# Gate h of a pair takes the reset state into its seven products, in a five-step gated graph network on one core

## The chip, the core and the metric

The kernel runs on one core of a Trainium2 chip. A core has five engines that run their own instruction streams and meet through semaphores: TensorE (PE in the profile: matrix products from SBUF into PSUM banks), VectorE (DVE), ScalarE (ACT), GpSimd (POOL) and SyncE (SP, which here issues most of the DMA transfers). The metric is the device time of one execution in microseconds (us), as a median over runs; lower is better.

## The reference, cut to what matters

The state has 2048 nodes with 256 features, and five steps of this loop run, followed by a small output layer and a layer norm:

```
s_in = state @ in_W.T + in_b;  s_out = state @ out_W.T + out_b
a_in = A @ s_in;  a_out = A.T @ s_out;  a = [a_in, a_out, state]
r = sigmoid(a @ r_W.T + r_b);  z = sigmoid(a @ z_W.T + z_b)
h = tanh([a_in, a_out, r * state] @ h_W.T + h_b)
state = (1 - z) * state + z * h
```

## The kernel before

The state is kept transposed (`state_t`, features on the partitions) in two feature halves of 128 and four chunks of 512 nodes. A float operand goes to PE as two fp16 parts, a high and a low one: ACT makes the high part, DVE the low part, and PE multiplies the three pairs high-high, high-low and low-high (`PASSES`). So each product of a 128x128 weight block with a 128x512 operand block is three matmuls.

Step 0 and the last two chunks of step 4 take the gates chunk by chunk (L1911). All other work takes two neighbouring chunks as a **pair**: (t, p) is step t, pair p, and there are seven of them, (1,0), (1,1), (2,0), (2,1), (3,0), (3,1) and (4,0). In a step, `group(t, g)` (L1792) makes the adjacency products of one direction and one pair by seven products P1 to P7 of 16 matmuls each in place of eight (the Strassen-Winograd scheme on 2x2 blocks); sums of their results, on ACT and DVE, give the operands `yop` (`y_sum`, `y_lo` L1390, `y_hi` L739).

`pair_gate(t, p, gate)` then makes the four PSUM tiles of gate r, z or h of a pair: two feature halves times two chunks, the tiles s = 0 to 3 of `PAIR_TILES`. It uses the same scheme on the weights: product y11 (called P1) into tile 0, t2 (P6) into tile 1, t1 (P5) into tile 2, t3 (P7) into tile 3, and then y21 into tile 0, y22 into tile 1 and t4 into tile 3. The inner dimension has three parts: the two adjacency results d = 0 and d = 1, and the state. For gates r and z, `pair_product` gives each of the seven products 3 state matmuls (L1924, from `sop`) and 6 matmuls of d = 0 and 1 (L1932), 63 in all. For gate h the third part is r * state. There the seven products hold only their 6 matmuls of d = 0 and 1, and `pair_state` (L1943) adds r * state to each of the four tiles by plain products, 6 matmuls per tile: 42 + 24 = 66.

Between the products the tiles are combined. ACT copies P1 (`pair_copy` L791), DVE adds (`pair_sum_u` L1553 after P6, `pair_sum_12` L1559 after P5, `pair_sum_22` L1564 and L1566 after P7), ACT writes the base of tile 3 (`pair_base_21` L795), and then the last products come. In gate h, tiles are finished in the order 1, 2, 0, 3 (`PAIR_ORDER[2]`). While PE makes gate z, ACT applies the sigmoid to gate r (L806), DVE multiplies by the state (`pair_reset` L1572), ACT makes the high part (`pair_reset_hi` L813) and DVE the low part (`pair_reset_lo` L1579). Gate h's banks are those of gate r: ACT seeds them with a bias term (`pair_seed` L783) and DVE adds the second term (`pair_degree` L1544) before PE may add to them (`s_c1`). After gate h, ACT applies the tanh (L806) and DVE updates the state (`pair_keep` L1587, `pair_update` L1596 and L1599).

At the end of a step (after pair p = 1) the new rows of the state are split (`rows_hi` L623, L631, L638; `row_sums` L1126 to L1131; `rows_lo` L1101, L1104, L1108) and SP transposes them by DMA into `xop` (`turn` L441), three parts for each chunk: part 0 after L1101, part 1 after L638, part 2 after L1108. Chunk 3 comes first, then chunk 2. The next step's `first_group` starts on the chunks 0 and 1, which are there, and meets waits for the parts of the chunks 3 and 2 at fixed places: its first five products with four operand pairs each (two for P7) are 36 matmuls; then come P1, P6 and P5 on chunk 3 and P1 on chunk 2. Its products also overwrite the banks of the gates just made: bank 0 held tile 1 of z, bank 3 tile 2, bank 2 tile 0, bank 7 tile 3, and bank 1 tile 3 of h. So P1, P5, P3 and P7 wait until z * h has read those (`s_zh`), and P6 until the tanh of tile 3 has (`s_act`).

Nothing is scheduled by a planner: each engine runs its instructions in the order in which they are written.

Of the kernel before, what the change touches and what calls it, by code (L numbers as in the profile page):

```python
# [19 lines left out]
FT = D // P  # L20
JT = N // P
CW = 512
# [33 lines left out]
PAIR_ORDER = ((0, 1, 2, 3), (1, 2, 0, 3), (1, 2, 0, 3))  # L56

# [12 lines left out]
def gnn_program(nc, x, x_t, adj, adj_t, io_w, gate_w, o_w, bias, o2_b, out):  # L70
    ctx = ExitStack()
    with ctx:
# [60 lines left out]
        h_pair = (sum_v, sum_1, sum_u, sum_u)  # L133
        xsum_b = pq_words[:, slot_words + 3 * CW:slot_words + 5 * CW]
# [21 lines left out]
        rs_pair = tmp[:, 4 * CW:8 * CW].bitcast(F16).rearrange("p (c s f n) -> p c s f n", c=2, s=2, f=FT)  # L156
# [65 lines left out]
        s_rs, s_rsh, s_rsl = sem("s_rs"), sem("s_rsh"), sem("s_rsl")  # L222
# [57 lines left out]
        def pair_index(t, p):  # L280
            return 2 * (t - 1) + p

# [88 lines left out]
        def _(sp):  # L371
# [170 lines left out]
        def _(act):  # L542
# [254 lines left out]
            def pair_act(t, p, gate, i):  # L797
# [4 lines left out]
                if gate < 2 and s == 2:  # L802
# [6 lines left out]
            def pair_reset_hi(t, p, i):  # L809
                s = PAIR_ORDER[0][i]  # L810
                f, c = PAIR_TILES[s]
                act.wait_ge(s_rs, FT * pair_at(t, p) + i + 1)
                nc.scalar.activation(rs_pair[:, c, 0, f, :], r_pair[:, s, :], ACT.Identity, scale=SIGX) \  # L813
                    .then_inc(s_rsh, 1)

            def pair_gates(t, p):
# [109 lines left out]
        def _(dve):  # L926
# [218 lines left out]
            def reset_lo(n, f):  # L1145
                dve.wait_ge(s_rsh, FT * n + f + 1)
# [3 lines left out]
            def keep_part(n, c, f):  # L1150
                dve.wait_ge(s_act, GT * n + 2 + f + 1)
                dve.wait_ge(s_rsl, FT * n + f + 1)
# [422 lines left out]
            def pair_reset_lo(t, p, i):  # L1575
                s = PAIR_ORDER[0][i]
                f, c = PAIR_TILES[s]
                dve.wait_ge(s_rsh, FT * pair_at(t, p) + i + 1)
                nc.vector.scalar_tensor_tensor(rs_pair[:, c, 1, f, :], r_pair[:, s, :], SIGX, rs_pair[:, c, 0, f, :],  # L1579
# [509 lines left out]
```

## Time and profile before

| | |
|---|---|
| median of 3 runs (lowest, highest) | 989.48 us (988.64, 991.54) |
| the profiled execution's own time | 987.27 us |
| its span, first to last instruction | 985.5 us, clock 0.997 of full speed |
| PE busy | 965.1 us (98%), 4480 matmuls |
| DVE busy | 735.6 us (75%) |
| ACT busy | 457.0 us (46%) |
| POOL busy | 35.8 us (4%) |

A matmul is shown 379 ns long, but the next one starts before it ends, so the busy time of PE tells that it had work and not how fast it went; how fast is read from the distance between starts. A timeline row gives the start, the length of the whole merged piece (for xN equal instructions), and in brackets how long the engine was idle before it and what released it.

### The profile page before, as it was taken

What the parts mean: (1) busy time and instruction counts of PE and PEld (TensorE: products, weight loads), DVE (VectorE), ACT (ScalarE), POOL (GpSimd) and SP (SyncE); (2) the same over time, 40 slices, a digit from 0 to 9 for tenths busy, and PEclk for the clock granted to TensorE, in tenths of its full rate; (3) what the DMA queues carried; (4) which work ended last, traced back from release to release, by engine and by line L of the source; (5) the groups of instructions that cost most, each with busy time, mean ns of one, the idle gap of its engine ahead of it and who ended that gap; (6) DMA issues with size and microseconds to landing.
All of it is one profiled execution on the core that took longest, in us unless ns stands there. A gap on an engine that the chain in (4) does not pass through costs nothing.

```text
span 985.5 us, 11893 instructions
## 1 busy us (share of the span) xinstructions
PE 965.1 (98%) x4480; PEld 441.2 (45%) x4480; DVE 735.6 (75%) x1157; ACT 457.0 (46%) x640; POOL 35.8 (4%) x43
## 2 busy tenths in 40 slices
PE   7999999999999999999999999999999999999995
PEld 3444444444444444444444444444444444445443
DVE  4999999888876688767668775876676687645756
ACT  4667665553354246433534552463345335412443
POOL 0311100000000000000000000000000100001100
PEclk9999999999999999999999999999999999999998
DMA  9999993324810454383035617601570681032101
GB/s 342 393 416 370 395 328 102 81 60 109 224 52 1 131 152 93 59 206 110 1 86 151 137 20 166 184 5 43 150 172 12 146 221 55 1 112 81 44 1 43
DMA packets 199784, 134.34 MB, mean 136 GB/s; under 512 B 62256, under 2 KB 191920, under 8 KB 195760
## 3 DMA queue, kind: packets, MB, share of 16 engines
q1 hardware_dynamic: 197424, 125.20, 44.1%
q0 software_dynamic: 2304, 8.39, 2.2%
q8 instruction: 36, 0.59, 0.2%
q14 instruction: 20, 0.16, 0.0%
HBM read 102.11 MB, written 16.78 MB: 121 GB/s over the span
## 4 chain that ended last, share of the span: by engine, by line
PE 91%; DVE 5%; ACT 2%; issue 1%; DMA 0%; ACTq 0%; SPq 0%; DVEq 0%
PE bank L1792 35%; PE bank L1932 19%; PE bank L1911 12%; PE bank L1717 11%; PE bank L1924 6%; PE bank L1943 4%; PE bank L1711 1%; PE bank L2003 1%; PE bank L2024 1%; ACT areg L739 1%; DVE pq_words L1354 0%; DVE pq_words L1347 0%; DVE pq_words L1341 0%; DMA pq_words<-in_gate_w 0%; DVE pq_words L1108 0%
## 5 line engine op out<-in xcount | busy, mean ns | idle before, releaser
L1792 PE MATMUL bank<-areg,xop_words 128*128 128x512 fp8e4 x1792 | 389.4, 379 | 0.8 <-DVE pq_words L1354 0.8
L1792 PEld LDWEIGHTS bank<-areg,xop_words 128*128 128x128 f16 x1792 | 174.9, 98 | 212.9 <-DVE pq_words L1354 2.7
L739 ACT ACTIVATE areg<-pq_words 128x512 f16<-128x512 f32 x90 | 56.3, 629 | 163.8 <-DVE pq_words L1354 62.7
L1932 PE MATMUL bank<-areg,pq_words 128*128 128x512 f16 x504 | 119.2, 379 | 0.7 <-DVE areg L1390 0.7
L1717 PE MATMUL bank<-areg,xop_words 128*128 128x512 fp8e4 x512 | 111.5, 379 | 1.8 <-ACT areg L555 1.8
L1932 PE MATMUL bank<-areg,w 128*128 128x512 f16 x378 | 90.9, 379 | 1.4 <-DVE areg L1390 1.4
L1390 DVE SCALAR_TENSOR_TENSOR areg<-pq_words,areg 128x512 f16<-128x512 f32 x90 | 62.2, 691 | 32.4 <-ACT areg L739 30.6
L1717 PEld LDWEIGHTS bank<-areg,xop_words 128*128 128x128 f16 x512 | 50.0, 98 | 62.4 <-issue 2.2
L1932 PEld LDWEIGHTS bank<-areg,pq_words 128*128 128x128 f16 x504 | 49.3, 98 | 60.4 <-DVE areg L1390 1.2
L565 ACT ACTIVATE areg<-tmp 128x2048 fp8e4<-128x2048 int32 x31 | 59.2, 1909 | 31.1 <-DMA tmp<-in_adj_t 17.2
L1911 PE MATMUL bank<-pq_words,w 128*128 128x512 f16 x288 | 65.4, 379 | 0.0
L1932 PEld LDWEIGHTS bank<-areg,w 128*128 128x128 f16 x378 | 36.9, 98 | 46.3 <-DVE areg L1390 1.9
L646 ACT ACTIVATE tmp<-bank,bias_sb,scal 128x512 f32<-128x512 f32 x36 | 27.8, 772 | 44.9 <-PE bank L1911 44.9
L1924 PE MATMUL bank<-sop_words,wss 128*128 128x512 f16 x168 | 45.4, 379 | 0.0
L1911 PEld LDWEIGHTS bank<-pq_words,w 128*128 128x128 f16 x288 | 28.2, 98 | 34.0
L806 ACT ACTIVATE bank<-bank,bias_sb,scal 128x512 f32<-128x512 f32 x56 | 40.1, 733 | 3.3 <-PE bank L1932 3.3
L1943 PE MATMUL bank<-tmp,w 128*128 128x512 f16 x168 | 39.7, 379 | 0.0
L795 ACT COPY bank<-pq_words 128x512 f32<-128x512 f32 x21 | 12.4, 590 | 58.2 <-DVE pq_words L1564 58.2
L537 POOL TENSOR_TENSOR areg<-areg,diag_words 128x256 f32<-128x256 f32 x16 | 13.0, 843 | 694.2 <-DMA areg<-in_x 694.2
L1596 DVE TENSOR_TENSOR pq_words<-bank,pq_words 128x512 f32<-128x512 f32 x28 | 19.3, 688 | 23.1 <-ACT pq_words L806 23.1
L1911 PE MATMUL bank<-sop_words,w 128*128 128x512 f16 x144 | 35.0, 379 | 0.9 <-DVE bank L1136 0.9
L1579 DVE SCALAR_TENSOR_TENSOR tmp<-tmp,scal 128x512 f16<-128x512 f32 x28 | 21.0, 751 | 17.7 <-ACT tmp L813 17.7
(214 smaller groups left out, 1208.3 us busy)
## 6 DMA issues: line engine op xcount, KB each, us to landing
areg<-kept_operands SPq DMA_DIRECT2D x112, 512.0 KB, 4.3
tmp<-in_adj_t SPq DMA_DIRECT2D x16, 1024.0 KB, 8.0
tmp<-in_adj SPq DMA_DIRECT2D x15, 1024.0 KB, 7.0
kept_operands<-xop_words POOLq DMA_DIRECT2D x11, 512.0 KB, 8.1
kept_operands<-areg SPq DMA_DIRECT2D x4, 1024.0 KB, 10.4
areg<-in_x SPq DMA_DIRECT2D x7, 512.0 KB, 6.1
kept_operands<-tmp POOLq DMA_DIRECT2D x5, 512.0 KB, 3.2
pq_words<-in_gate_w SPq DMA_DIRECT2D x6, 384.0 KB, 5.4
```

The source lines that it names most:

```text
L565: nc.scalar.activation(raw8[k // JT][:, k % JT, :], stage[:, k % STG, :], ACT.Copy, accum_out=degc[:, k // JT, k % JT:k % JT + 1], saturat ...
L646: nc.scalar.activation(dst[:, gi % FT, :], gate_bank[gi % 3][:, :], ACT.Tanh if gi >= 2 * FT else ACT.Sigmoid, bias=bias_sb[:, 4 + gi:5 + ...
L739: nc.scalar.activation(y_dst(t, g, name)[:, 0, :], src, ACT.Copy, scale=PSC).then_inc(s_yh, 1)
L806: nc.scalar.activation(h_pair[s] if gate == 2 else slot, slot, ACT.Tanh if gate == 2 else ACT.Sigmoid, bias=bias_sb[:, 4 + gi:5 + gi], sca ...
L1390: nc.vector.scalar_tensor_tensor(rows[:, 1, :], src, PSC, rows[:, 0, :], ALU.mult, ALU.subtract).then_inc(s_yl, 1)
L1579: nc.vector.scalar_tensor_tensor(rs_pair[:, c, 1, f, :], r_pair[:, s, :], SIGX, rs_pair[:, c, 0, f, :], ALU.mult, ALU.subtract).then_inc(s ...
L1717: return nc.tensor.matmul(dst[:, :], state_n[:, j, part, feat(f)], adj8[:, j, cols(c)], start=j == 0 and part == 0, stop=j == JT - 1 and p ...
L1792: last = nc.tensor.matmul(dst[:, :], xop[:, m // 2, operand_block(xo, part, m % 2), :], place8[:, mo, m, :], start=first and m == pairs[0] ...
L1911: last = nc.tensor.matmul(dst[:, :], w16[:, k, wp, feat(gi)], rhs, start=False, stop=i == KT - 1 and (wp, xp) == PASSES[-1], skip_group_ch ...
L1924: nc.tensor.matmul(dst[:, :], weights(2, wp), sop[:, Y_PLACE[name], xp, :], start=False, stop=False, skip_group_check=True)
L1932: last = nc.tensor.matmul(dst[:, :], weights(d, wp), yop[:, d, Y_PLACE[name], xp, :], start=False, stop=final and d == 1 and (wp, xp) == P ...
L1943: last = nc.tensor.matmul(pair_banks[2][s][:, :], w16[:, 2 * FT + k, wp, feat(2 * FT + f)], rs_pair[:, c, xp, k, :], start=False, stop=k = ...
```

## The change

The seven products of gate h each take a third part of 3 matmuls, as those of the gates r and z do, from seven operands of the reset state b = r * state: y11, y21 and y22 are three of its tiles, t1 = b12 - b11, t3 = b22 - b12, t2 = b22 - t1 and t4 = b21 - t2. `pair_state` is gone. DVE makes the four sums (`pair_reset_sum`), and high and low parts are made for six items in the order `RS_ORDER`, where t1 and t2 are one item of 1024 columns. The new operands lie in `tmp` and in two stretches of `areg` into which the rows of x are loaded for the residual at the end. So that load (`load_rest` 0 and 1) now waits for the last pair's gate h and stands behind `load_group(14)` in SP's order. In `first_group`, P6 moves behind P5 and P3. In gate r of pair (1,0) the opening products come in the order t3, y11, t2, t1. The keeps of DVE are interleaved with the sums of gate h.

```diff
+RS_ORDER = ("y11", "y22", "t12", "t3", "y21", "t4")
+        rs_at = {"y11": rs_block[:, 0], "y22": rs_block[:, 1], "y21": rs_block[:, 2], "t4": rs_block[:, 3],
+                 "t1": rs_t12[:, 0], "t2": rs_t12[:, 1], "t3": rs_t3}
...
                 if t == LAST:
...
-                    load_rest(0)
-                    load_rest(1)
                 for at in range(4 * (t - 1) + 1, 4 * t + 1):
+                    if at == 4 * LAST - 1:
+                        sp.wait_ge(s_gate, GT * (CH * LAST + 2))
+                        load_rest(0)
+                        load_rest(1)
...
             def pair_gates(t, p):            # ScalarE
...
-                for i in range(3):
+                pair_act(t, p, 0, 0)
+                pair_reset_hi(t, p, "y11")
+                for i in range(1, 4):
                     pair_act(t, p, 0, i)
-                    pair_reset_hi(t, p, i)
-                pair_act(t, p, 0, 3)
                 pair_copy(t, p, 1)
-                pair_reset_hi(t, p, 3)
+                pair_reset_hi(t, p, "y22")
+                pair_reset_hi(t, p, "t12")
+                pair_reset_hi(t, p, "t3")
+                pair_reset_hi(t, p, "y21")
                 pair_seed(t, p, 2, 0)
+                pair_reset_hi(t, p, "t4")
                 pair_base_21(t, p, 1)
...
             def first_group(t):              # TensorE
...
-                if t > 1:
-                    pe.wait_ge(s_act, GT * pair_at(t - 1, 1) + 12)
-                product(bank_b, at, XS2, MT2, early, final=False)
                 if t > 1:
                     pe.wait_ge(s_zh, zs + 2)
                 product(bank_e, at, XS1, MT1, early, final=False)
                 if t > 1:
                     pe.wait_ge(s_zh, zs + 3)
                 product(bank_c, at, XS4, M22, early, final=False)
+                if t > 1:
+                    pe.wait_ge(s_act, GT * pair_at(t - 1, 1) + 12)
+                product(bank_b, at, XS2, MT2, early, final=False)
...
             def pair_product(t, p, gate, dst, name, weights, final=False):
...
+                if gate == 2:
+                    half_name = "t12" if name in ("t1", "t2") else name
+                    pe.wait_ge(s_rsl, rs_before(pair_at(t, p)) + RS_ORDER.index(half_name) + 1)
+                    for wp, xp in PASSES:
+                        last = nc.tensor.matmul(dst[:, :], weights(2, wp), rs_at[name][:, xp, :], start=False,
+                                                stop=final and (wp, xp) == PASSES[-1], skip_group_check=True)
                 return last
-            def pair_state(t, p, s):
...
```

**PE in gate h of the first pair.** Bank 5 is tile 1, bank 6 tile 2, bank 4 tile 0 and bank 1 tile 3. Before, from the opening product t1 on:

```order
L1932 MATMUL bank6<-areg,pq_words 128x512 x6
L1932 MATMUL bank1<-areg,pq_words 128x512 x6
L1932 MATMUL bank5<-areg,pq_words 128x512 x6
L1943 MATMUL bank5<-tmp,w16 128x512 x6
L1943 MATMUL bank6<-tmp,w16 128x512 x6
L1932 MATMUL bank4<-areg,w16 128x512 x6
L1943 MATMUL bank4<-tmp,w16 128x512 x6
L1932 MATMUL bank1<-areg,w16 128x512 x6
L1943 MATMUL bank1<-tmp,w16 128x512 x6
```

In the changed kernel, from the same product on:

```order
L2000 MATMUL bank6<-areg,pq_words 128x512 x6
L2008 MATMUL bank6<-areg,wss 128x512 x3
L2000 MATMUL bank1<-areg,pq_words 128x512 x6
L2008 MATMUL bank1<-areg,wss 128x512 x3
L2000 MATMUL bank5<-areg,pq_words 128x512 x6
L2008 MATMUL bank5<-tmp,wss 128x512 x3
L2000 MATMUL bank4<-areg,w16 128x512 x6
L2008 MATMUL bank4<-tmp,w16 128x512 x3
L2000 MATMUL bank1<-areg,w16 128x512 x6
L2008 MATMUL bank1<-tmp,w16 128x512 x3
```

The reset state has moved from the end of each tile into every product. Tile 1 (bank 5) was complete 30 matmuls before the end of the gate, tile 2 24 and tile 0 12 before it; now both tile 1 and tile 2 are complete 18 before it, tile 0 9 before it.

**PE in `first_group` of step 2**, right behind gate h of pair (1,1), with the semaphores waited for. Before:

```order
L1792 MATMUL bank0<-areg,xop_words 128x512 [waits s_zh,s_place0,s_turn01,s_turn00]
L1792 MATMUL bank0<-areg,xop_words 128x512 x7
L1792 MATMUL bank1<-areg,xop_words 128x512 [waits s_turn21,s_act,s_turn20,s_place4,s_turn11,s_turn10]
L1792 MATMUL bank1<-areg,xop_words 128x512 x7
L1792 MATMUL bank3<-areg,xop_words 128x512 [waits s_place3,s_zh]
L1792 MATMUL bank3<-areg,xop_words 128x512 x7
L1792 MATMUL bank2<-areg,xop_words 128x512 [waits s_place2,s_zh]
L1792 MATMUL bank2<-areg,xop_words 128x512 x7
```

In the changed kernel:

```order
L1859 MATMUL bank0<-areg,xop_words 128x512 [waits s_zh,s_place0,s_turn01,s_turn00]
L1859 MATMUL bank0<-areg,xop_words 128x512 x7
L1859 MATMUL bank3<-areg,xop_words 128x512 [waits s_turn21,s_zh,s_turn20,s_place3,s_turn11,s_turn10]
L1859 MATMUL bank3<-areg,xop_words 128x512 x7
L1859 MATMUL bank2<-areg,xop_words 128x512 [waits s_place2,s_zh]
L1859 MATMUL bank2<-areg,xop_words 128x512 x7
L1859 MATMUL bank1<-areg,xop_words 128x512 [waits s_place4,s_act]
L1859 MATMUL bank1<-areg,xop_words 128x512 x7
```

The product that waits for the tanh of tile 3 (bank 1, `s_act`) has moved from the 9th matmul to the 25th. What follows, and the places of the later waits for the transposes, is as it was.

**DVE while PE makes gate z of the first pair.** L1572 is `pair_reset`, L1579 `pair_reset_lo`, L1553 and L1559 are the sums after P6 and P5. Before:

```order
L1572 TENSOR_TENSOR tmp<-bank4,state_t 128x512
L1579 SCALAR_TENSOR_TENSOR tmp<-tmp,scal 128x512
L1572 TENSOR_TENSOR tmp<-bank5,state_t 128x512
L1579 SCALAR_TENSOR_TENSOR tmp<-tmp,scal 128x512
L1572 TENSOR_TENSOR tmp<-bank6,state_t 128x512
L1579 SCALAR_TENSOR_TENSOR tmp<-tmp,scal 128x512
L1572 TENSOR_TENSOR tmp<-bank1,state_t 128x512
L1553 TENSOR_TENSOR pq_words<-bank0,pq_words 128x512
L1579 SCALAR_TENSOR_TENSOR tmp<-tmp,scal 128x512
L1559 TENSOR_TENSOR bank0<-bank3,pq_words 128x512
```

In the changed kernel (L1605 is `pair_reset`, L1635 `pair_reset_lo`, L1586 and L1592 the two sums, L1615 to L1625 `pair_reset_sum`):

```order
L1605 TENSOR_TENSOR tmp<-bank4,state_t 128x512
L1635 SCALAR_TENSOR_TENSOR tmp<-tmp,scal 128x512
L1605 TENSOR_TENSOR tmp<-bank5,state_t 128x512
L1615 TENSOR_TENSOR pq_words<-tmp 128x512
L1605 TENSOR_TENSOR tmp<-bank6,state_t 128x512
L1618 TENSOR_TENSOR pq_words<-tmp 128x512
L1621 TENSOR_TENSOR pq_words<-tmp,pq_words 128x512
L1605 TENSOR_TENSOR tmp<-bank1,state_t 128x512
L1586 TENSOR_TENSOR pq_words<-bank0,pq_words 128x512
L1592 TENSOR_TENSOR bank0<-bank3,pq_words 128x512
L1635 SCALAR_TENSOR_TENSOR tmp<-tmp,scal 128x512
L1625 TENSOR_TENSOR tmp<-tmp,pq_words 128x512
```

Up to the sum after P5 the same number of instructions stands: three low parts have made way for three sums, and the low parts come later, between the seeds' second terms of gate h.

## Rows read from the trace of the kernel before

**Rows 1.** The page: span, engines, and the plain state products of gate h.

```profile
span 985.5 us, 11893 instructions
PE 965.1 (98%) x4480; PEld 441.2 (45%) x4480; DVE 735.6 (75%) x1157; ACT 457.0 (46%) x640; POOL 35.8 (4%) x43
...
L1943 PE MATMUL bank<-tmp,w 128*128 128x512 f16 x168 | 39.7, 379 | 0.0
```

**Rows 2.** Chain that ended last: a stretch of gate products.

```profile
393.15 7.77 PE bank L1932 x36
```

**Rows 3.** Timeline of PE, opening of gate r of pair (1,0).

```profile
274.87 0.81 PE L1924 MATMUL bank<-sop_words,w 128*128 128x512 f16 x3
...
277.75 0.82 PE L1932 MATMUL bank<-areg,w 128*128 128x512 f16 x3 [1.43 <-DVE areg L1390]
...
280.53 0.82 PE L1932 MATMUL bank<-areg,pq_words 128*128 128x512 f16 x3 [0.66 <-DVE areg L1390]
```

**Rows 4.** Timeline of DVE beside it.

```profile
274.75 1.75 DVE L1465 TENSOR_TENSOR pq_words<-tmp,pq_words 128x1536 f16<-128x1536 f32 x1
...
277.01 0.68 DVE L1390 SCALAR_TENSOR_TENSOR areg<-bank,areg 128x512 f16<-128x512 f32 x1
...
279.78 0.69 DVE L1390 SCALAR_TENSOR_TENSOR areg<-pq_words,areg 128x512 f16<-128x512 f32 x1 [0.69 <-ACT areg L739]
...
283.58 0.69 DVE L1559 TENSOR_TENSOR bank<-bank,pq_words 128x512 f32<-128x512 f32 x1
```

**Rows 5.** Timeline of PE, pair (1,1): gate z begins, gate h inside, step 2 begins.

```profile
380.69 0.81 PE L1924 MATMUL bank<-sop_words,w 128*128 128x512 f16 x3
...
392.99 2.75 PE L1932 MATMUL bank<-areg,w 128*128 128x512 f16 x12
...
408.53 20.88 PE L1792 MATMUL bank<-areg,xop_words 128*128 128x512 fp8e4 x96
```

**Rows 6.** Timeline of DVE, pair (1,1), during gate z.

```profile
379.02 0.68 DVE L1572 TENSOR_TENSOR tmp<-bank,state_t 128x512 f32<-128x512 f32 x1
...
387.59 0.69 DVE L1559 TENSOR_TENSOR bank<-bank,pq_words 128x512 f32<-128x512 f32 x1
```

**Rows 7.** Timeline of ACT, pair (1,1): last sigmoid of r, first and last tanh of h.

```profile
384.65 0.73 ACT L806 ACTIVATE bank<-bank,bias_sb,scal 128x512 f32<-128x512 f32 x1
...
402.26 0.78 ACT L806 ACTIVATE pq_words<-bank,bias_sb,scal 128x512 f32<-128x512 f32 x1 [1.28 <-PE bank L1943]
...
409.03 0.76 ACT L806 ACTIVATE pq_words<-bank,bias_sb,scal 128x512 f32<-128x512 f32 x1
```

**Rows 8.** Timeline of DVE, pair (1,1): updates of the state and low parts.

```profile
403.07 0.69 DVE L1596 TENSOR_TENSOR pq_words<-bank,pq_words 128x512 f32<-128x512 f32 x1 [1.98 <-ACT pq_words L806]
...
409.58 1.28 DVE L1108 SCALAR_TENSOR_TENSOR pq_words<-diag_words,scal,pq_words 128x1024 f16<-128x1024 f32 x1
```

**Rows 9.** Transposes of chunk 3 part 2 (issued 410.9) and chunk 2 part 0 (412.9).

```profile
L441 SPq DMA_TRANSPOSE xop_words<-pq_words x1: 1350/1350/1350, 410.9 to 410.9; - x1
DMA to landing us min/median/max: 3.4/3.4/3.4
...
L441 SPq DMA_TRANSPOSE xop_words<-tmp x1: 1232/1232/1232, 412.9 to 412.9; - x1
DMA to landing us min/median/max: 3.0/3.0/3.0
```

**Rows 10.** The same part 2 of chunk 3 at the end of step 3; PE's step 4 begins.

```profile
L441 SPq DMA_TRANSPOSE xop_words<-pq_words x1: 1349/1349/1349, 770.8 to 770.8; - x1
DMA to landing us min/median/max: 3.7/3.7/3.7
...
768.40 0.81 PE L1792 MATMUL bank<-areg,xop_words 128*128 128x512 fp8e4 x3
```

**Rows 11.** POOL's additions to the rows of x; a DVE split behind pair (4,0).

```profile
784.38 5.50 POOL L537 TENSOR_TENSOR areg<-areg,diag_words 128x256 f32<-128x256 f32 x8 [554.97 <-DMA areg<-in_x]
...
862.19 2.48 DVE L1076 SCALAR_TENSOR_TENSOR sop_words<-state_t,scal,sop_words 128x1024 f16<-128x1024 f32 x2 [1.22 <-ACT sop_words L594]
```

More of the change, by code:

```diff
@@ L133, in gnn_program @@
         h_pair = (sum_v, sum_1, sum_u, sum_u)
+        rs_sums_12 = pq_words[:, slot_words:slot_words + 2 * CW].rearrange("p (i n) -> p i n", i=2)
         xsum_b = pq_words[:, slot_words + 3 * CW:slot_words + 5 * CW]
@@ L281, in pair_index, with rs_before @@
             return 2 * (t - 1) + p
+        def rs_before(n):
+            t, c = n // CH, n % CH
+            if t == 0:
+                return FT * n
+            pairs = 2 * (t - 1) + (1 if c >= 2 else 0)
+            return FT * CH + len(RS_ORDER) * pairs + (FT * (c - 2) if t == LAST and c > 2 else 0)
         def state_done(n, f):
@@ L801, in pair_act @@
                 act.wait_ge(s_gate, GT * n + 4 * gate + i + 1)
-                if gate < 2 and s == 2:
+                if s == 2:
                     act.wait_ge(s_g22, pair_unit(t, p, gate) + 1)
@@ L807, in pair_act, with pair_reset_hi @@
                                      bias=bias_sb[:, 4 + gi:5 + gi], scale=UG).then_inc(s_act, 1)
[L809 to L814, printed above, removed]
+            def pair_reset_hi(t, p, name):
+                n, sums = pair_at(t, p), 4 * pair_index(t, p)
+                if name in ("y11", "y22", "y21"):
+                    tile = {"y11": 0, "y22": 2, "y21": 3}[name]
+                    act.wait_ge(s_rs, FT * n + tile + 1)
+                    src, dst = r_pair[:, tile, :], rs_at[name][:, 0, :]
+                elif name == "t12":
+                    act.wait_ge(s_rt, sums + 3)
+                    src, dst = rs_sums_12, rs_t12[:, :, 0, :]
+                elif name == "t3":
+                    act.wait_ge(s_rt, sums + 2)
+                    src, dst = sum_v, rs_t3[:, 0, :]
+                else:
+                    act.wait_ge(s_rt, sums + 4)
+                    src, dst = r_pair[:, 1, :], rs_at["t4"][:, 0, :]
+                nc.scalar.activation(dst, src, ACT.Identity, scale=SIGX).then_inc(s_rsh, 1)
             def pair_gates(t, p):
@@ L1573, in pair_reset, with pair_reset_sum, pair_reset_lo @@
                                         ALU.mult).then_inc(s_rs, 1)
[L1575 to L1579, printed above, removed]
-                                               ALU.mult, ALU.subtract).then_inc(s_rsl, 1)
+            def pair_reset_sum(t, p, name):
+                n, first = pair_at(t, p), 4 * pair_index(t, p)
+                b11, b12, b22, b21 = [r_pair[:, i, :] for i in range(4)]
+                if name == "t1":
+                    dve.wait_ge(s_rs, FT * n + 2)
+                    nc.vector.tensor_tensor(sum_1, b12, b11, ALU.subtract).then_inc(s_rt, 1)
+                elif name == "t3":
+                    dve.wait_ge(s_rs, FT * n + 3)
+                    nc.vector.tensor_tensor(sum_v, b22, b12, ALU.subtract).then_inc(s_rt, 1)
+                elif name == "t2":
+                    dve.wait_ge(s_rt, first + 1)
+                    nc.vector.tensor_tensor(sum_u, b22, sum_1, ALU.subtract).then_inc(s_rt, 1)
+                else:
+                    dve.wait_ge(s_rs, FT * n + 4)
+                    dve.wait_ge(s_rt, first + 3)
+                    nc.vector.tensor_tensor(b12, b21, sum_u, ALU.subtract).then_inc(s_rt, 1)
+            def pair_reset_lo(t, p, name):
+                dve.wait_ge(s_rsh, rs_before(pair_at(t, p)) + RS_ORDER.index(name) + 1)
+                if name == "t12":
+                    src, hi, lo = rs_sums_12, rs_t12[:, :, 0, :], rs_t12[:, :, 1, :]
+                else:
+                    src = {"y11": r_pair[:, 0, :], "y22": r_pair[:, 2, :], "y21": r_pair[:, 3, :],
+                           "t3": sum_v, "t4": r_pair[:, 1, :]}[name]
+                    hi, lo = rs_at[name][:, 0, :], rs_at[name][:, 1, :]
+                nc.vector.scalar_tensor_tensor(lo, src, SIGX, hi, ALU.mult, ALU.subtract).then_inc(s_rsl, 1)
             def pair_keep(t, p, i):
@@ L1902, in gate_tile @@
                     if k >= 2 * FT and gi == 2 * FT:
[L1903 removed]
+                        pe.wait_ge(s_rsl, rs_before(n) + k - 2 * FT + 1)
                     for wp, xp in PASSES:
```

92 lines of the change are left out of this document (45 added, 47 removed).

## The prediction

> **What bounds the kernel now.** I read the page first. PE is busy for 98% of the span and all 4480 matmuls are its own; DVE, the next, has 75% [rows 1]. A matmul is shown 379 ns long, yet 36 gate products in a row take 7.77 us in the chain that ended last, so PE starts one every 7.77 / 36 = 0.2158 us [rows 2]. That pace, and not the 379 ns, is what a matmul costs when it has none but other matmuls beside it. From the start of step 1 to the output layer the chain is PE almost without a break. The waits of PE then tell where it stood still in the stages that the diff touches: nowhere except in gate r of pair (1,0), where two products waited for low parts made on DVE, with 1.43 and 0.66 us idle [rows 3]. So the change is worth the matmuls that it saves, plus what it takes from these two waits, less any wait that it makes. The last is read from the timelines of DVE, ACT and the transposes around one pair: (1,1), since its end also carries the transposes.
>
> **Term 1, the matmuls.** `pair_state` issues 168 matmuls [rows 1] = 7 pairs x 24. Gate h now takes 7 x 3 = 21 in their place, 3 fewer for each pair, 21 in all: 21 x 0.2158 = **4.53 us** off. The form and width of the matmuls are those of the neighbours, so I keep the pace.
>
> **Term 2, the opening of gate r in pair (1,0).** Before, y11 is first. Its state part starts at 274.87, 6 matmuls run, and d = 1 waits for the low part that DVE starts at 277.01; t2's d = 1 waits for the one that ends at 279.78 + 0.69 = 280.47 [rows 3, 4]. By starts, PE lost 277.75 - (274.87 + 6 x 0.2158) = 1.59 us and 280.53 - (277.75 + 9 x 0.2158) = 0.84 us, 2.43 together. Now t3 opens. Its own low part precedes 274.75 in DVE's order, but its d = 1 also needs the low weights of L1465, 274.75 + 1.75 = 276.50 [rows 4], where PE is ready at 276.16: a wait of about 0.4. Then 3 + 6 matmuls bring it to 277.85, y11's low part is there since 277.69, and t2's d = 1 comes at 278.50 + 6 x 0.2158 = 280.45 against 280.47: 0.05. The gain is 2.43 - 0.45 = **1.95 us**. What covered the sums before was t3 behind t1. Now t1 ends at 280.53 + 12 x 0.2158 = 283.12, and the sum that follows (L1559) runs at 283.58 to 284.27 [rows 4]; but y21 stands between, which does not need it and keeps PE until 285.06. No wait. Gate z starts 1.95 us earlier while DVE cannot come that much earlier, so its first reset is some 0.8 us later against PE than in other pairs; the next term shows the room.
>
> **Term 3, the new work on DVE and ACT in gate z: nothing, with bounds.** Per pair DVE gets four sums of 0.69 us and, for low parts, five of 0.75 and one of 1.28 us (the 1024 columns of L1108 [rows 8]) in place of four of 0.75: 2.8 + 2.0 = 4.8 us more. What must not be late are three things. First, the sum after P5, which y22 of gate z needs. Gate z starts at 380.69 and y22 comes 36 matmuls in, at 388.46 [rows 5]. Of the changed order, seven instructions stand between the second reset (which waits for a sigmoid and starts near 381.2) and that sum; at 0.61 to 0.72 us from start to start they end by 386.2, and P5 itself ends at 380.69 + 26 x 0.2158 + 0.38 = 386.68. So the sum runs at 386.7 to 387.4, no later than its 387.59 before [rows 6], with 1.05 us in hand; the 0.8 us of pair (1,0) are absorbed too, since P5 still comes last. Second, the sigmoids: before, each waited for a high part in between and the last one ran at 384.65 [rows 7]; now they run together, which is why the sums can follow. Third, gate h's openings: low parts and second seed terms alternate until about 395.9. Gate h starts at 392.99 + 6 x 0.2158 = 394.28; y11 is ready, t1 and t2's low part is done near 391.3 and needed 15 matmuls in, at 397.5, and the last seed term is needed 27 in, at 400.1. The least room is 2.3 us. I take 0. The bounds: not below 0 (PE has no wait there to lose), and at most the full 4.8 us in each of 7 pairs, were none of it hidden, 34 us, which the rows make remote.
>
> **Term 4, the end of a pair.** Tile 1 of h was complete after 36 matmuls of gate h and its tanh began at 402.26 [rows 7] (394.28 + 35 x 0.2158 + 0.38 = 402.21). Now it is the 45th: 394.28 + 44 x 0.2158 + 0.38 = 404.16, so the tanh starts at 404.20, 1.94 later, and everything chained to it moves by the same, while PE ends the gate 3 matmuls sooner, at 407.88 in place of 408.53 [rows 5]. Against PE the chain comes 12 matmuls, 2.59 us, later. Within a step (after p = 0) PE needs the first z * h at once, and it is there at 403.07 + 0.69 + 1.94 = 405.7 [rows 8]. The tanh of tile 3 ends near 408.9 on this clock, needed 16 matmuls in. Nothing.
>
> Between steps (after p = 1, three times) ACT and DVE also split rows. The tanh of tile 3 moves from 409.03 + 0.76 = 409.79 [rows 7] to 411.73. In the old place P6 would have stood at 407.88 + 8 x 0.2158 = 409.61 and lost 2.1 us at each of three ends, 6.4 in all; in the new one it stands at 413.06. P5 and P3 come forward to 409.61 and 411.33; they need z * h of tiles 2 and 0, which by DVE's order end near 407.0 and 410.5. P7 at 414.79 needs tile 3's, behind L1108: 409.58 + 1.28 + 1.94 + 0.7 = 413.5 [rows 8]. All met. Next the transposes, which no edit moved. Part 2 of chunk 3 landed at 410.9 + 3.4 = 414.3 [rows 9]; P6's matmul on it is the 41st, and its weights are loaded one matmul ahead: needed at 408.53 + 39 x 0.2158 = 416.95, 2.65 in hand, of which 0.06 is left. Part 0 of chunk 2 landed at 412.9 + 3.0 = 415.9 [rows 9], needed at 408.53 + 47 x 0.2158 = 418.67: 2.8, of which 0.2 is left. At the end of step 3 the landing took 3.7: 770.8 + 3.7 = 774.5 against 768.40 + 39 x 0.2158 = 776.82 [rows 10], so 0.3 is missing. With the time in which a semaphore is seen I take **0.3 us** of new wait over the three ends; bounds 0 and, with each landing as late as the slowest seen (the 3.7), 0.9.
>
> **Term 5, the rows of x.** Their load and POOL's additions move from about 780 to about 854, where SP waits for the last gate h and nothing behind it in the queue is due before a group has passed. The additions took 5.50 us for eight [rows 11] and are needed some 20 us later. I take 0.
>
> The Trainium skill speaks against this move (SBUF — State Buffer, "SBUF: two separate sides"): GpSimd and a DVE instruction with two SBUF inputs take one port pair as an exclusive lock, the later one waiting out the other's whole instruction. No row of before shows such a pair at once. Near 862 stand two splits of that kind (`state_t`, `sop_words`) [rows 11] whose first feeds PE's hidden layer about 2 us after it ends; held up by an addition of 5.50 / 8 = 0.69 us each, three such DVE instructions come 2.1 late, so by the page the sum would be 0.1 us longer, and without it the same.
>
> **The sum.** 985.5 - 4.53 - 1.95 + 0.3 = 979.3 us of span, 6.2 less. The profiled execution took 987.27, so 981.1. The median of the runs is 989.48, 2.2 above the profiled one; taking 6.2 from it gives **983.3 us**. Its own range is 982 to 985.
>
> **The rivals.** (a) The step-1 gain does not come, because the weights' low part or the sum behind P5 is late: only term 1 and 0.3 remain, 4.2 off, 985.3. For it: term 2 hangs on two DVE ends with 0.02 and 0.2 us of room. Against: each is a matter of tenths. (b) The transposes are the new bound: the row sums of ACT and DVE take 1 us longer in the new neighbourhood, or landings stretch. Each us costs three, so 1.2 us make -6.2 + 3.6 = -2.6: 986.9. For it: the room of 0.06 us. Against: the chain of instructions is the same and only starts later. (c) Slower: DVE falls behind in gate z. The sum after P5 has 1.05 us of room; beyond it each us costs 7, once a pair. Break-even is at 1.05 + 6.2 / 7 = 1.9 us late; 3 us late (DVE kept from packing the seven instructions, at 1.1 in place of 0.7 us each) gives -6.2 + 7 x 1.95 = +7.5: 997. For it: 4.8 us of new work. Against: most of that work stands behind the critical sum. (d) The change does not do what it says, the lost matmuls being given back by waits for operands of the reset state within gate h: no change, 989.5. Against: 2.3 us of least room.
>
> **Chances.** Forecast 0.68, (a) 0.12, (b) 0.10, (c) 0.04, (d) 0.06. The range for 8 in 10 reaches from the forecast's lower edge, with the runs' own scatter, to case (a): 981.2 to 986.4. A difference under 0.3% (3 us) cannot be told from none. Faster by more is below 986.5: forecast, (a) and half of (b), with a little lost to scatter, 0.86. Within it: half of (b), (d), 0.09. Slower: (c) and a rest, 0.05.
>
> **What would show it.** 4459 matmuls; pairs' gate h 63 starts long with no gap; in pair (1,0) a first wait of 0.4 us for L1465's successor and almost none for t2; the tanh of tile 1 9.9 us after gate h's start, before 8.0; P6 at the 25th matmul without a wait for ACT; short waits for transposes at the 41st or 49th. The forecast is wrong if PE waits more than 1 us in all for DVE within gates z and h, or more than 0.5 at one end of a step.

## The result, and the profile after

The changed kernel takes 982.29 us (median of 5 runs, 981.11 to 982.39) against 989.20 us (5 runs, 987.92 to 991.54): a ratio of 0.9925, 95% interval 0.9907 to 0.9943, so 0.6 to 0.9% faster. The prediction said 983.3 us with a range of 981.2 to 986.4. The span of the profiled execution is 979.6 us where 979.3 was worked out, and was 985.5 before [rows 1].

The page of the changed kernel, its head and two lines:

```profile
span 979.6 us, 11914 instructions
...
PE 959.9 (98%) x4459; PEld 438.7 (45%) x4459; DVE 765.9 (78%) x1199; ACT 468.3 (48%) x654; POOL 37.6 (4%) x43
```

PE has 4459 matmuls, 21 fewer. DVE has 42 more instructions and 30.3 us more work, 4.3 us per pair where 4.8 was worked out (busy time counts the overlap of neighbouring instructions once), and it still is not what bounds. The groups by line, each form apart, show the third parts of gate h, 147 = 7 pairs x 21, with no idle time before them (the last column), where L1943 had 168 [rows 1]:

```profile
L2008 PE MATMUL bank<-areg,wss 128*128 128x512 f16 x63 | 17.0, 379 | 0.0
L2008 PE MATMUL bank<-tmp,w 128*128 128x512 f16 x63 | 17.0, 379 | 0.0
L2008 PE MATMUL bank<-tmp,wss 128*128 128x512 f16 x21 | 5.7, 379 | 0.0
```

The opening of gate r in pair (1,0), timeline of PE, then of DVE:

```profile
275.10 0.81 PE L1992 MATMUL bank<-sop_words,wss 128*128 128x512 f16 x3
275.75 0.81 PE L2000 MATMUL bank<-areg,pq_words 128*128 128x512 f16 x3
276.88 0.81 PE L2000 MATMUL bank<-areg,pq_words 128*128 128x512 f16 x3 [0.32 <-DVE pq_words L1498]
...
280.11 1.47 PE L2000 MATMUL bank<-areg,pq_words 128*128 128x512 f16 x6
```

```profile
274.98 1.75 DVE L1498 TENSOR_TENSOR pq_words<-tmp,pq_words 128x1536 f16<-128x1536 f32 x1
...
280.01 0.69 DVE L1423 SCALAR_TENSOR_TENSOR areg<-pq_words,areg 128x512 f16<-128x512 f32 x1 [0.69 <-ACT areg L757]
```

DVE runs as before [rows 4], 0.23 us later on the clock of the span; only what PE asks of it has changed. One wait is left, for the weights' low part (274.98 + 1.75 = 276.73, PE goes on at 276.88): 276.88 - (275.10 + 6 x 0.2158) = 0.48 us by starts. The two of before were 1.59 and 0.84 [rows 3]. The one for t2's low part, which ends at 280.70, is down to 0.01: PE was there at 280.76.

Pair (1,1) and the beginning of step 2, timeline of PE (the same rows as [rows 5], with y22 of gate z and of gate h between):

```profile
378.33 0.81 PE L1992 MATMUL bank<-sop_words,w 128*128 128x512 f16 x3
...
386.10 0.81 PE L1992 MATMUL bank<-sop_words,wss 128*128 128x512 f16 x3
...
390.63 2.75 PE L2000 MATMUL bank<-areg,w 128*128 128x512 f16 x12
...
400.99 0.81 PE L2008 MATMUL bank<-tmp,wss 128*128 128x512 f16 x3
```

The same stretch on DVE (sum after P5 in gate z, then low parts and second seed terms) and on ACT (tanh of tiles 1 and 2, tanh of tile 3):

```profile
384.36 0.70 DVE L1592 TENSOR_TENSOR bank<-bank,pq_words 128x512 f32<-128x512 f32 x1 [1.01 <-PE bank L2000]
...
392.79 0.75 DVE L1577 SCALAR_TENSOR_TENSOR bank<-deg_words,vdif,bank 128x512 f32<-128x512 f16 x1
```

```profile
401.84 1.45 ACT L824 ACTIVATE pq_words<-bank,bias_sb,scal 128x512 f32<-128x512 f32 x2 [0.63 <-PE bank L2008]
...
408.61 0.76 ACT L824 ACTIVATE pq_words<-bank,bias_sb,scal 128x512 f32<-128x512 f32 x1
```

Gate h starts at 390.63 + 6 x 0.2158 = 391.92; it ends where step 2 begins, at 405.52: 13.60 us, 63 starts at 0.2158 with nothing between. The sum after P5 is done at 385.06 and y22 of gate z stands at 386.10: 1.04 us of room, and DVE waits 1.01 us for P5 before it. The last seed term ends at 393.5. The closest of them is the first, which ends at 389.58, 2.3 us before gate h starts. The tanh of tile 1 begins 9.92 us into gate h (before: 402.26 - 394.28 = 7.98).

The transposes of chunk 3 part 2 and of chunk 2 part 0 at that place (issue, time to landing), and PE's first products of step 2 in one piece, once cut behind the 39th start and once behind the 41st:

```profile
L457 SPq DMA_TRANSPOSE xop_words<-pq_words x1: 1347/1347/1347, 410.5 to 410.5; - x1
DMA to landing us min/median/max: 3.6/3.6/3.6
...
L457 SPq DMA_TRANSPOSE xop_words<-tmp x1: 1231/1231/1231, 412.5 to 412.5; - x1
DMA to landing us min/median/max: 3.1/3.1/3.1
```

```profile
405.52 8.58 PE L1859 MATMUL bank<-areg,xop_words 128*128 128x512 fp8e4 x39
...
405.52 9.10 PE L1859 MATMUL bank<-areg,xop_words 128*128 128x512 fp8e4 x41
```

39 starts take 38 x 0.2158 + 0.38 = 8.58, as shown; 41 would take 9.01 and are shown with 9.10. The difference, 0.09 us, is the wait for part 2, which landed at 410.5 + 3.6 = 414.1, where the weights of the 41st matmul would have been loaded at 405.52 + 39 x 0.2158 = 413.94. At the ends of steps 2 and 3 there is none.

**A stretch that can be compared.** The profiled executions differ by up to 2.4 us in what comes before the first gate (131.7 to 134.1 us): PE begins later or earlier, waits for DVE and ACT before and in the adjacency products of step 0 for 2 to 4 us, and in three of the fourteen makes some eight of the first of these at half pace. The diff touches nothing there. So the traces are compared by the stretch from the first gate matmul of step 0 to the end of the last matmul, with the distances between starts of all matmuls in it. Before it is 976.30 - 131.72 = 844.6 us, after 970.14 - 131.96 = 838.2: 6.4 off, which is 4.53 + 1.95 - 0.09. The span shows 5.8 (985.48 and 979.65), because the beginning took 0.24 and the tail behind the last matmul 0.34 more.

### The profile page after: what moved, and what is told of

Read it like the earlier page. It is cut to its first block, busy times and chain, and to the rows that moved or that the text cites. A ratio compares the mean times of both kernels' runs of the same rounds, so it can differ in the third digit from the quotient of the medians.

```text
span 979.6 us, 11914 instructions
## 1 busy us (share of the span) xinstructions
PE 959.9 (98%) x4459; PEld 438.7 (45%) x4459; DVE 765.9 (78%) x1199; ACT 468.3 (48%) x654; POOL 37.6 (4%) x43
## 4 chain that ended last, share of the span: by engine, by line
PE 90%; DVE 5%; ACT 2%; issue 2%; DMA 1%; SPq 1%; ACTq 0%; POOL 0%; DVEq 0%
PE bank L1859 36%; PE bank L2000 19%; PE bank L1978 12%; PE bank L1784 11%; PE bank L1992 6%; PE bank L2008 3%; PE bank L2081 1%; PE bank L2060 1%; DMA areg<-in_x 1%; ACT areg L757 0%; DVE pq_words L1387 0%; DVE pq_words L1380 0%; DVE pq_words L1374 0%; DVE xop_words L983 0%; DVE mx L969 0%
## 5 line engine op out<-in xcount | busy, mean ns | idle before, releaser
L2000 PE MATMUL bank<-areg,pq_words 128*128 128x512 f16 x504 | 122.7, 379 | 0.3 <-DVE pq_words L1498 0.3
L2000 PE MATMUL bank<-areg,w 128*128 128x512 f16 x378 | 90.7, 379 | 0.0
L1978 PE MATMUL bank<-sop_words,w 128*128 128x512 f16 x144 | 35.0, 379 | 0.9 <-DVE bank L1169 0.9
L1992 PE MATMUL bank<-sop_words,w 128*128 128x512 f16 x126 | 34.0, 379 | 0.0
L1978 PE MATMUL bank<-areg,w 128*128 128x512 f16 x144 | 32.9, 379 | 0.0
L1169 DVE SCALAR_TENSOR_TENSOR bank<-deg_words,vdeg,bank 128x512 f32<-128x512 f16 x36 | 26.8, 751 | 4.9 <-ACT bank L678 4.8
```

Source lines behind the costliest of these rows:

```text
L1169: nc.vector.scalar_tensor_tensor(slot, deg[:, 1, cols(c)], vdeg[:, 1, gi:gi + 1], slot, ALU.mult, ALU.add).then_inc(s_c1, 1)
L1978: last = nc.tensor.matmul(dst[:, :], w16[:, k, wp, feat(gi)], rhs, start=False, stop=i == KT - 1 and (wp, xp) == PASSES[-1], skip_group_ch ...
L1992: nc.tensor.matmul(dst[:, :], weights(2, wp), sop[:, Y_PLACE[name], xp, :], start=False, stop=False, skip_group_check=True)
L2000: last = nc.tensor.matmul(dst[:, :], weights(d, wp), yop[:, d, Y_PLACE[name], xp, :], start=False, stop=final and gate < 2 and d == 1 and ...
```

## The experiments

Each kernel's own median and its ratio to the kernel before, run on the same chip beside it (95% interval), and the stretch defined above from its one profiled execution. The median of the kernel before lay between 988.5 and 989.2 us in these comparisons.

| kernel | median us | ratio to before | stretch us |
|---|---|---|---|
| before | 989.2 | | 844.6 |
| changed | 982.3 | 0.9907 to 0.9943 | 838.2 |
| changed, again | 983.2 | 0.9921 to 0.9954 | 838.1 |
| P6 second again | 990.6 | 1.0007 to 1.0036 | 846.8 |
| old opening | 985.0 | 0.9942 to 0.9975 | 840.3 |
| before, new opening alone | 987.1 | 0.9970 to 0.9992 | 843.4 |
| before, 21 matmuls left out | 984.5 | 0.9938 to 0.9968 | 840.0 |
| changed, 3 fillers | 983.7 | 0.9927 to 0.9966 | 838.7 |
| changed, 5 fillers | 990.8 | 1.0013 to 1.0041 | 846.0 |
| changed, 1 filler at the end | 984.2 | 0.9934 to 0.9979 | 839.8 |
| changed, P3 later | 980.5 | 0.9898 to 0.9940 | 836.2 |
| changed, weights first | 982.6 | 0.9917 to 0.9947 | 837.6 |
| changed, both | 982.7 | 0.9916 to 0.9951 | 836.4 |
| P3 later, additions later | 980.4 | 0.9896 to 0.9935 | 836.2 |

**21 matmuls by themselves.** In the kernel before:

```diff
                 for k in range(FT):
+                    if s == 1 and k == 0:
+                        continue
```

> The kernel before, with gate h as it was but the three state matmuls of one of the two inner blocks of tile 1 left out in each of the seven pairs (so that part of r * state does not enter tile 1 of h). It prices 21 matmuls by themselves: no sums, no other order, no other operands. Theory: 21 x 0.2158 = 4.5 us off (span 981.0). Rival: a matmul that goes gives its shown 379 ns, 8.0 us off; or part of it is lost to waits for ACT and DVE, which do not get faster: under 4 us off.

4459 matmuls, and the stretch is 4.55 us shorter (844.58 to 840.03). The 21 matmuls of term 1 are worth 21 starts, nothing more and nothing less. The two waits in the opening are the same to 0.01 us, and so are four others that all kernels up to here have: in the first group of each of the steps 1 to 4, PE waits 0.35 us before the product P4 for its operand y22. The 379 ns reading is out.

**The opening alone, and taken back.** The condition `(t, p, gate) == (1, 0, 0)` set to false in the changed kernel, and its branch put into the kernel before.

> The changed kernel, but gate r of pair (1,0) opens with y11, t2, t1, t3 as everywhere. Theory: the two waits of PE for DVE's low parts come back (1.59 and 0.83 us by starts) in place of one of 0.48: 1.95 us slower than the changed kernel, -4.2 against before. Rival: the changed order only moves a wait to a later place of the same gate, since DVE's order is the same; then no difference from the changed kernel (-6).

The two waits are back at the same places with 1.59 and 0.82 us, that of 0.48 is gone, and the stretch is 2.1 us longer: 1.93, and 0.16 of a wait for the transposes at the end of step 3.

> The kernel before, with only the new opening of gate r in pair (1,0): t3, y11, t2, t1. Theory: 1.95 us off (span 983.5), with one wait of 0.48 us left in that gate. Rival as above: 0 off.

This one missed by its trace (the runs, 0.1 to 0.3% faster, fit 1.2 and 1.95 alike). The opening gives its 1.95 us (one wait of 0.48 is left), but the stretch is only 1.2 us shorter. A new wait of 0.72 us by starts stands in gate z of the same pair, timeline of PE and of DVE:

```profile
298.06 0.82 PE L1924 MATMUL bank<-sop_words,wss 128*128 128x512 f16 x3 [0.56 <-DVE bank L1559]
```

```profile
288.74 0.68 DVE L1572 TENSOR_TENSOR tmp<-bank,state_t 128x512 f32<-128x512 f32 x1
...
296.64 0.75 DVE L1579 SCALAR_TENSOR_TENSOR tmp<-tmp,scal 128x512 f16<-128x512 f32 x1 [0.19 <-ACT tmp L813]
297.31 0.69 DVE L1559 TENSOR_TENSOR bank<-bank,pq_words 128x512 f32<-128x512 f32 x1
```

With the gates' old order on DVE the sum after P5 comes 8.57 us after the first reset (288.74 to 297.31; before, in pair (1,1), 379.02 to 387.59 [rows 6]), since each reset waits for a high part in between. In the changed kernel it comes when P5 is there, 384.36 in pair (1,1) and 295.22 in pair (1,0), there with only 0.17 us of idle time before it. So the new opening pays in full only together with the new order on DVE; 0.7 of its 1.95 us are the order's.

**P6 back in second place in `first_group`** (the diff's block undone).

> The changed kernel, but in the first group of a step the product P6 stands second again, as before the change. Theory: P6 waits for the tanh of tile 3 of h, which now ends at 409.37 on the changed kernel's clock, while P6 would stand at 407.25. So PE waits some 2.1 us at the ends of steps 1, 2 and 3, and the small wait of 0.09 us for the transposes at the first of them goes: 6.2 us slower than the changed kernel, about as slow as before (-6.2 + 6.2 = 0 against before). Rival: the three later products need their own z * h no earlier than P6 needs the tanh, so the move only renames the wait; then this kernel is within 0.5 us of the changed one (-6 against before).

The wait for the tanh is there at all three ends, 2.40, 2.38 and 2.37 us by starts. Timeline of PE at the ends of step 1 and step 2:

```profile
405.80 1.89 PE L1859 MATMUL bank<-areg,xop_words 128*128 128x512 fp8e4 x8
409.93 5.39 PE L1859 MATMUL bank<-areg,xop_words 128*128 128x512 fp8e4 x17 [2.24 <-ACT pq_words L824]
...
592.50 7.71 PE L1859 MATMUL bank<-areg,xop_words 128*128 128x512 fp8e4 x35 [2.21 <-ACT pq_words L824]
```

The three waits make 7.15 us, more than the 6.3 expected: the tanh ended at 409.65 and PE went on only at 409.93, 0.28 us later, where 0.06 passed between the end of DVE's sum and y22 in the waits in gate z. And at the first of them 1.5 us more were lost behind the wait: eight matmuls started 0.43 us apart, not 0.2158. The table by stretches (columns: length, busy time and count of PE, weight loads, DVE, ACT, POOL, then the granted clock, DMA share, GB/s):

```profile
407.00:409.80 2.80, 0.69 (x4) 0.10 (x1) 2.73 (x7) 1.97 (x3) 0.00 (x0) 0.98 0.49 94
409.80:413.10 3.30, 3.17 (x8) 1.20 (x9) 3.27 (x6) 0.97 (x2) 0.00 (x0) 0.50 0.92 172
413.10:416.50 3.40, 3.40 (x17) 1.51 (x16) 2.15 (x5) 2.29 (x4) 0.00 (x0) 1.00 0.54 103
```

The granted clock is 0.50 (the level of 1.2 GHz) for 3.3 us behind the idle time and full (2.4 GHz) after. Behind the two equal waits at the other ends it stayed full. The stretch is 8.6 us longer than the changed kernel's: without the move of P6 the change would have given nothing; by the runs that kernel is 0.1 to 0.4% slower than before. The rival falls: in the changed kernel P5 and P3, which came forward, wait for nothing, and neither does P7.

**How much room DVE has in gate z.** A maximum over 512 columns, written to unused words, is put between the sums after P6 and P5, three times and five times:

```diff
                 pair_sum_u(t, p, 1)
+                filler(3)
                 pair_sum_12(t, p, 1)
```

> The changed kernel with three more instructions of about 0.58 us from start to start (a maximum over 512 columns, not used) on DVE in every gate z, between the sums after P6 and P5: 1.75 us more. Theory: in six pairs DVE is idle for 1.0 us before the sum after P5 and that sum ends 1.0 us before y22 needs it, 2.0 us of room, so they lose nothing; in pair (1,0) DVE is idle only 0.17 us, 1.2 us of room, so 0.5 us is lost. In all +0.5 us against the changed kernel. Rival (DVE is at its limit in gate z): every pair pays, 7 x 1.75 = +12 us.

Of the seven pairs only (1,0) waits, 0.53 us by starts, and the stretch is 0.5 us longer. Its line in the view of PE's waits (us in all, times, longest; idle time, so less than by starts):

```profile
PE bank L2002 <- DVE bank L1593: 0.4, 1, 0.4
```

> As the one with three, but five: 2.9 us more on DVE in every gate z. Theory: beyond the room, 6 x 0.9 + 1.7 = +7 us against the changed kernel, with the wait of PE at y22 of gate z. Rival (at its limit): +20 us; and if there is far more room than 2 us: 0.

Now all seven wait: 1.71 us in pair (1,0), and 0.87 or 0.88 in each of the others. DVE and PE in pair (1,1):

```profile
385.95 3.05 DVE L1664 TENSOR_REDUCE tmp<-state_t 128x1 f32<-128x512 f32 x5
388.92 0.69 DVE L1593 TENSOR_TENSOR bank<-bank,pq_words 128x512 f32<-128x512 f32 x1
```

```profile
389.67 0.82 PE L2002 MATMUL bank<-sop_words,wss 128*128 128x512 f16 x3 [0.71 <-DVE bank L1593]
```

The stretch is 7.8 us longer, 7.0 of these waits and 0.8 of one for the transposes at the end of step 3. Six pairs have 2.0 us of room at the critical sum, pair (1,0) has 1.2, and behind it every us costs seven. That is rival (c) of the prediction with its price confirmed, and its condition not met.

**How much room the transposes have.** One such instruction ahead of `row_sums(CH * t + 2)`.

> The changed kernel with one more such instruction (0.58 us from start to start) on DVE at the ends of steps 1 to 3, ahead of the row sums of chunk 3. Theory: the transposes of that chunk land within 0.1 us of where PE needs them, so the chain passes on what is added: waits of 0.5 to 0.7 us at the 41st matmul of the first groups of steps 2, 3 and 4, +1.6 us in all. Rival: the transposes still have room and the 0.09 us seen is a wait for something else: no wait at that place, +0.

At the 41st matmul of the three first groups PE waits 0.51, 0.69 and 0.49 us by starts; the timeline of PE at two of the ends (the profile names no releaser here, "issue"):

```profile
416.07 2.10 PE L1869 MATMUL bank<-areg,xop_words 128*128 128x512 fp8e4 x9 [0.35 <-issue]
...
595.39 1.89 PE L1869 MATMUL bank<-areg,xop_words 128*128 128x512 fp8e4 x8 [0.53 <-issue]
```

The stretch is 1.6 us longer, as expected: the room that the change left is used up. Over all other variants with the changed gate h and P6 in its new place, the ends of steps show waits of 0 to 0.16 us at this place and, once, 0.81 (five fillers, end of step 3). They go with the time that part 2 of chunk 3 took to land: 3.4 us with 0 to 0.06, 3.6 with 0.09 (changed kernel, end of step 1), 3.7 with 0.16 (old opening, end of step 3) and 4.3 with the 0.81. So small differences in landing now reach PE.

**What is left, and a faster version.** Three variants take up the waits that remain in the touched stages. "P3 later" moves four matmuls of P3 (the operand pairs `next_rows`, in step 1 the last two of `early`) from before P2 to behind P7, "weights first" swaps two calls on DVE in step 1, "both" has both:

```diff
-                product(bank_c, at, XS4, M22, early, final=False)
+                product(bank_c, at, XS4, M22, early[:-2] if t == 1 else early, final=False)
...
                 if t > 1:
                     product(bank_f, at, XS3, MT3, next_rows, first=False, final=False)
-                    product(bank_c, at, XS4, M22, next_rows, first=False, final=False)
...
                 product(bank_f, at, XS3, MT3, late, first=False).then_inc(s_p7, 1)
+                product(bank_c, at, XS4, M22, next_rows or early[-2:], first=False, final=False)
                 product(bank_c, at, XS4, M22, late, first=False).then_inc(s_p3, 1)
...
                     y_sum(t, g, "t3")
-                    y_lo(t, g, "t3")
                     if t == 1 and g == 1:
                         weight_lo(1)
+                    y_lo(t, g, "t3")
```

> The changed kernel again, beside the three variants that follow. Theory: span 979.6 +- 0.5, -6.2 us against before; it gives the scatter of the tail, which in its first profile was 0.3 us longer than before's.

> The changed kernel, with four matmuls of P3 in each first group of a step moved from before P2 to behind P7. Theory: the 0.35 us waits before P4 (for the sum y22, after P6, P5 and P7) are covered by the four matmuls moved (0.86 us), in all four first groups: -1.4 us against the changed kernel. Rival: P2 and the waits for the transposes come four matmuls earlier, and one of them (the copy of P1, or part 1 and 2 of chunk 2) starts to wait: 0 or more.

> The changed kernel, with the low part of the second weight sums (1.75 us) ahead of the low part of t3 on DVE in step 1, where DVE is idle for 0.7 us. Theory: the wait of 0.48 us that is left in the opening of gate r goes: -0.5 us against the changed kernel. Rival: the low part of t3, now behind it, becomes late in its place: 0.

> Both of the last two edits in the changed kernel. Theory: they are in different stages and add up, -1.9 us against the changed kernel, -8.1 against before (span 977.7). Rival: less than either alone if they share a cover.

The changed kernel again has the same waits as at first, without the 0.09 at the end of step 1. P3 later takes 2.0 us off the stretch, more than expected: all four waits before P4 are gone (4 x 0.35), the one of 0.48 in the opening too, and the 0.09 at the end of step 1. The timeline of PE shows one piece where it was cut:

```profile
276.75 1.46 PE L2000 MATMUL bank<-areg,pq_words 128*128 128x512 f16 x6
```

```profile
275.48 1.75 DVE L1498 TENSOR_TENSOR pq_words<-tmp,pq_words 128x1536 f16<-128x1536 f32 x1
```

P6, P5 and P7 of the first group end four matmuls earlier, 0.86 us, of which PE itself takes back 0.35; DVE, which from there on works without much idle time up to the weights, is 0.5 us earlier against PE. Weights first takes 0.6 off, its wait of 0.48 gone and the 0.09 absent. Both together are no better than P3 later alone (836.4 against 836.2, with 0.23 us of waits for transposes): they shared a cover, so the rival was right there. Against the same runs of the kernel before, P3 later has 0.9919 and the changed kernel 0.9938 with overlapping intervals; by the runs alone the two cannot be told apart, by the stretches of one trace each they can, and the second kernel with this edit, below, has 836.2 again. (The median of "both", 982.7, is 2.2 above that of P3 later, with overlapping intervals too; the stretch does not show it.)

**The additions of POOL moved into DVE's idle time**, on top of P3 later:

```diff
             pool.wait_ge(s_b2, 16)
+            pool.wait_ge(s_u4, 4 * LAST - 1)
```

> The changed kernel with the four matmuls of P3 moved, and POOL's additions to the rows of x held back until the third sum of step 4's third group (DVE, near 869 on the changed kernel's clock), where DVE has 4 us of idle time. Theory (each of two engines waits out the other's instruction when both read SBUF twice or as the skill's lock has it): the two splits behind pair (4,0) take 1.28 us each again (2.48 merged) in place of 2.95, the low part of the hidden layer 0.69 in place of 1.10, and the eight additions 5.5 us in place of 7.8. The time stays that of the kernel with P3 moved, -2.0 us against the changed one, because all of it was hidden. Rival: the stretching came from the DMA of the rows landing beside it; then the additions still take over 7 us or the time moves.

It answers what the additions did in their new place. In the changed kernel, timeline of POOL, and of DVE behind pair (4,0):

```profile
856.60 7.79 POOL L555 TENSOR_TENSOR areg<-areg,diag_words 128x256 f32<-128x256 f32 x8 [626.96 <-DMA areg<-in_x]
```

```profile
856.13 2.95 DVE L1109 SCALAR_TENSOR_TENSOR sop_words<-state_t,scal,sop_words 128x1024 f16<-128x1024 f32 x2 [1.22 <-ACT sop_words L612]
...
862.71 1.10 DVE L1283 SCALAR_TENSOR_TENSOR pq_words<-pq_words 128x512 f16<-128x512 f32 x1
```

With the additions later:

```profile
865.33 5.96 POOL L556 TENSOR_TENSOR areg<-areg,diag_words 128x256 f32<-128x256 f32 x8 [634.72 <-DVE pq_words L1381]
```

```profile
855.08 2.48 DVE L1110 SCALAR_TENSOR_TENSOR sop_words<-state_t,scal,sop_words 128x1024 f16<-128x1024 f32 x2 [1.22 <-ACT sop_words L613]
...
861.66 0.69 DVE L1284 SCALAR_TENSOR_TENSOR pq_words<-pq_words 128x512 f16<-128x512 f32 x1
```

Beside each other, the two splits of DVE take 2.95 us and eight additions 7.79; apart they take 2.48 and 5.96 (5.50 in the kernel before [rows 11]). So the two engines did hold each other up. One by one, in the changed kernel: the first split ran first (856.13, 1.28 us) and lost nothing; the first addition, begun beside it at 856.60, took 1.40 us; the second split took 1.75 and the second addition 1.70. With the additions later, one of them (869.43) again met a DVE instruction with two SBUF inputs (L1424, 869.33) and took 1.17, which is the difference between 5.96 and 5.50. The DMA of the rows is not the cause: with the additions later it was issued at 851.5 and 852.0 and landed 3.9 and 4.9 us after, beside the two splits as before, and both took 1.28 us. None of it reached PE: the stretch is 836.2 us with and without.

## Why the prediction was right

**Term 1** (4.53 us) measured 4.55 by itself. The choice that carried it was to price a matmul by the distance between starts.

**Term 2** (1.95 us) came out as 1.93 to 1.95 in the traces, the remaining waits as 0.48 and 0.01 where 0.4 and 0.05 were worked out. Two lines of its working are wrong as written: 9 matmuls, not 6, lie between 278.50 and t2's d = 1 (278.50 + 9 x 0.2158 = 280.44), and y11's d = 1, which takes the low part of 277.69, comes at 278.50 and not at 277.85. The results stand, and one of the two "rooms" of rival (a), the 0.2 us, was 0.8. Its step "no wait" in gate z was right for this kernel for the reason given, the resets packed behind the sigmoids; the opening by itself showed how much hung on it. The prediction priced the two edits apart and did not say that 0.7 us of the one depend on the other. Rival (a) is out.

**Term 3** (nothing) held in every pair. The sum after P5 was worked out for 386.7 to 387.4 with 1.05 us before its use, and ran with 1.04; the last seed term was worked out 1.6 us after gate h's start and ended 1.6 after it. Of the instructions that it put between the second reset and that sum there are six, not seven; the seventh is the reset itself, and the time of 386.2 includes it. The "least room" of 2.3 us came without its working, and the trace has 2.3 for the first seed term. Rivals (c) and (d) fail on these numbers: fillers of 3.05 us made the first one true at its price.

**Term 4.** The shift of 1.94 us is in the trace (9.92 - 7.98). The stay of P6 in its old place was priced at 6.4 us and measured 7.15 of waits and 1.5 behind one of them; the 0.28 us from the tanh to PE and the fall of the granted clock were not in it. The new wait was put at 0.3 us and is 0.09 in one trace and 0 in the next. The step 3 landing of 3.7 us, on which most of the 0.3 rested, did not recur in the changed kernel, where part 2 took 3.4 to 3.6; with the old opening it did, and PE waited 0.16 us. How large this term comes out is chance. Rival (b) did not come, though its condition is close: one instruction more of 0.58 us costs 1.6.

**Term 5.** Hidden, as taken. The Trainium skill's rule (SBUF — State Buffer, "SBUF: two separate sides") stands: the trace agrees, with the two splits stretched from 2.48 to 2.95 us and the additions from 5.50 to 7.79. The 0.1 us that the sum would have had by it did not come: the first split, which PE's hidden layer needs first, had begun 0.47 us before the first addition and lost nothing, the second lost 0.47 and the low part of the hidden layer 0.41, together 0.9 and not 2.1.

**The sum.** 979.3 against 979.6 of span. That is closer than the terms deserve, and luck: the stretch lost 6.4 where 6.18 was forecast, and the beginning and the tail, not forecast, took 0.6 back. The medians fell by 6.9 us, with 5.6 to 9.2 inside their interval, so the runs alone bear out the size only roughly. The chances of the cases counted as faster add up to 0.85, given as 0.86.

**Waits that it did not count.** The prediction says that PE stood still nowhere in the touched stages except in gate r of pair (1,0). The four waits of 0.35 us before P4, in `first_group`, were there too. They are the same before and after, so the sum is not touched, but they were worth more (1.4 us) than the wait left in gate r.

## What to carry to other kernels

In a kernel bound by one engine, price a removed instruction by the distance between starts, and then look for what moves against that engine: here the rest of the chain at the end of a pair came 12 matmuls (2.6 us) later against PE, and moving one product behind two others was worth more (7.15 us of waits) than the 21 matmuls themselves. Work that grows on a second engine was free here because what stood ahead of that engine's critical result in program order did not grow; fillers of known length, put at one place, tell the room in one or two runs. When two edits touch the same chain, try each alone: the gain of one may need the order that the other brings.

## What was not expected of the hardware

- PE idle for 2.4 us was followed by 3.3 us of half the granted clock (0.50) in one of three equal cases, and cost 1.5 us more than the wait. The half pace in step 0 is the same: PE waits 2.0 to 3.0 us before its first adjacency product in all fourteen traces, and in three of them (waits of 2.7, 2.3 and 2.4) the granted clock behind it is 0.50, in the others, with longer waits among them, 1.00. The waits of 0.3 to 1.7 us elsewhere were never followed by it.
- The time from the last matmul's start to the end of the span is 9.4 to 9.5 us in the traces of the kernel before, its two variants and the three with fillers, and 9.8 in the changed kernel and its other variants, though the code of that part is the same. In the latter DVE begins a residual of the last rows 0.35 us later against PE (0.04 us before the last matmul's start, in place of 0.39). In all eight of them, and in none of the other six, a load of instructions (queue q14, 8 KB) stands 0.6 us behind the last matmul's start. That is behind the late instruction, so it is not shown to be the reason; no run tested it, and it stays open.
